# Second attention layer: the row of maxima is placed ahead of the step's scores, and copied ahead of the step's exponent

## The reference, cut to what matters

```python
q = q * scale
attn = jnp.einsum('bqd,bkd->bqk', q, k)
attn = (attn.reshape(B * nh, H, W, H, W) + rel_h[:, :, :, :, None] + rel_w[:, :, :, None, :]).reshape(B * nh, N, N)
attn = jax.nn.softmax(attn, axis=-1)
out = jnp.einsum('bqk,bkd->bqd', attn, v)
...
x = x + _L0_conv_ref(_gn(x), ...)
x = x + _L1_conv_ref(_gn(x), ...)
```

## Time and profile before

| | us |
|---|---|
| median of 3 runs | 3359.76 |
| lowest, highest | 3355.78, 3362.64 |
| the profiled execution's own time | 3359.43 |
| its span, first to last instruction | 3357.2 |
| PE busy | 2895.1 (86%) |
| DVE busy | 2494.8 (74%) |
| POOL busy | 1903.2 (57%) |
| ACT busy | 1862.9 (55%) |

### The profile page before, as it was taken

One profiled execution on the slowest core, in us unless ns is written; L12 is line 12 of the kernel. 1 busy time (PEld: TensorE's weight loads), 2 busy tenths in 40 slices (PEclk: granted clock), 3 DMA queues, 4 the chain that ended last, 5 costly groups with the idle time before them and its releaser, 6 DMA issues. The chain is left out here.

```text
span 3357.2 us, 94851 instructions
## 1 busy us (share of the span) xinstructions
PE 2895.1 (86%) x34200; PEld 1947.2 (58%) x34200; DVE 2494.8 (74%) x5171; ACT 1862.9 (55%) x3434; POOL 1903.2 (57%) x1561
## 2 busy tenths in 40 slices
PE   1996999997199748999999999999999999999977
PEld 1554677773155625666666666666666666666644
DVE  6745888876654537888787888888888888888854
ACT  3333666774333425666565666656565666566654
POOL 3452555550303006777777777777777777777762
PEclk9996999998599559999999999999999999999989
DMA  2425565547121984222222222222222222222114
GB/s 115 178 87 132 139 145 132 139 117 258 45 119 58 245 185 136 49 50 50 50 50 50 50 50 50 50 50 53 47 58 48 56 49 56 46 57 59 22 41 142
DMA packets 162461, 294.95 MB, mean 88 GB/s; under 512 B 78522, under 2 KB 112404, under 8 KB 156564
## 3 DMA queue, kind: packets, MB, share of 16 engines
q1 hardware_dynamic: 162052, 289.43, 33.9%
HBM read 189.37 MB, written 85.45 MB: 82 GB/s over the span
## 5 line engine op out<-in xcount | busy, mean ns | idle before, releaser
L1704 POOL TENSOR_TENSOR fprob_low<-fprob 128x768 f16<-128x768 f32 x1008 | 1449.7, 1466 | 563.3 <-ACT fprob L1672 562.8
L1715 DVE TENSOR_REDUCE fpart_max<-fmax_acc 128x1 f32<-128x384 f32 x2592 | 1363.8, 556 | 368.7 <-PE fmax_acc L1543 353.0
L1672 ACT ACTIVATE fprob<-fscores 128x768 f32<-128x768 f32 x1296 | 1048.2, 809 | 768.7 <-PE fscores L1572 768.6
L1543 PE MATMUL fmax_acc<-fk_m,fq_m 128*128 128x384 f16 x2592 | 853.2, 330 | 146.0 <-ACT fq_b L1660 104.8
L1570 PE MATMUL fscores<-fq_a,fk_a 128*128 128x384 f16 x2592 | 848.2, 327 | 39.5 <-issue 31.5
L1572 PE MATMUL fscores<-fq_b,fk_b 97*128 97x384 f16 x2592 | 851.4, 328 | 4.2 <-issue 4.2
L1596 PE MATMUL fout_acc<-fv,fprob 128*128 128x65 f16 x7776 | 612.0, 191 | 2.6 <-POOL fprob_low L1704 2.1
L1597 PE MATMUL fout_acc<-fv,fprob_low 128*128 128x33 f16 x7776 | 596.0, 179 | 0.9 <-issue 0.9
L1596 PEld LDWEIGHTS fout_acc<-fv,fprob 128*128 128x128 bf16 x7776 | 543.2, 97 | 68.4 <-POOL fprob_low L1704 5.1
L1597 PEld LDWEIGHTS fout_acc<-fv,fprob_low 128*128 128x128 f16 x7776 | 487.9, 96 | 52.5 <-issue 2.6
L1543 PEld LDWEIGHTS fmax_acc<-fk_m,fq_m 128*128 128x128 f16 x2592 | 251.9, 97 | 336.7 <-DVE fpart_max L1715 121.1
(11 more groups left out here) (128 smaller groups left out, 3834.9 us busy)
## 6 DMA issues: line engine op xcount, KB each, us to landing
q_a<-q_hi SPq DMA_DIRECT2D x48, 432.0 KB, 5.7
fq_a<-q_hi SPq DMA_DIRECT2D x48, 432.0 KB, 7.6
q_a<-q_lo SPq DMA_DIRECT2D x24, 432.0 KB, 7.4
row_bias<-x SPq DMA_DIRECT2D x24, 432.0 KB, 7.7
col_bias<-x SPq DMA_DIRECT2D x72, 144.0 KB, 3.8
fq_a<-q_lo SPq DMA_DIRECT2D x24, 432.0 KB, 8.6
fq_a<-col_bias SPq DMA_DIRECT2D x24, 432.0 KB, 11.9
fq_b<-row_bias SPq DMA_DIRECT2D x24, 432.0 KB, 14.6
```

The source lines that it names most:

```text
L1543: nc.tensor.matmul(max_acc[:, piece_bank(g, u, j), 0:PIECE], q_m[:, b, tile * 128:(tile + 1) * 128], k_m[:, b, piece * PIECE:(piece + 1) * ...
L1672: nc.scalar.activation(prob[:, k % RING, :].rearrange("p (j n) -> p j n", j=2), scores[:, 2 * (k % 2):2 * (k % 2) + 2, 0:UNIT], ACT.Exp).t ...
L1704: engine.tensor_tensor(prob_low[:, k % RING, :], prob[:, k % RING, :], prob[:, k % RING, :].bitcast(BF16)[:, 1::2], ALU.subtract).then_inc ...
L1715: nc.vector.reduce_max(part_max[:, u % 2, j // PIECES, j % PIECES:j % PIECES + 1], max_acc[:, piece_bank(g, u, j), 0:PIECE], axis=AX.X).th ...
```

## The change

In `attention_full`, at step 7 of a unit, PE's `row_of_max` stands ahead of `scores_of` instead of behind it, and ACT's `place_row` stands ahead of `exps` instead of behind it. The waits are the same ones, written at the same operations. A function is renamed.

```diff
@@ PE, stage
                 for k in range(STEPS):
-                    scores_of(n, b, k)
-                    coming = row_after(n, k)
+                    coming = row_of(n, k)
                     if coming:
                         row_of_max(*coming)
+                    scores_of(n, b, k)
@@ ACT, stage
                 for k in range(STEPS):
-                    exps(n, k)
-                    coming = row_after(n, k)
+                    coming = row_of(n, k)
                     if coming:
                         place_row(*coming, b if coming[1] else 1 - b)
+                    exps(n, k)
```

More of the change, by code:

```diff
@@ L1433, in piece_bank, with row_of @@
         return (u + j + (1 if j < 2 else 0)) % 2
-    def row_after(n, k):
+    def row_of(n, k):
         unit = k // PAIRS + 1
```

## The result

| | before | after |
|---|---|---|
| median | 3361.2 us of 4 runs (3355.78 to 3367.49) | 3284.74 us of 4 runs (3281.58 to 3286.59) |
| the profiled execution's own time | 3359.43 us | 3281.58 us |
| its span | 3357.2 us | 3279.3 us |

The ratio is 0.9771, with a 95% interval of 0.9752 to 0.9790: the change makes the kernel faster by 76.5 us by the medians and by 77.9 us between the two profiled executions. Forecast were 79.8 us and 3280 us.

The account below looks back on a forecast made before the run. PE was taken to bound the kernel. Per unit 0.90 - 0.32 = 0.58 us; 132 x 0.58 + 10 x 0.32 = 79.8 us off 3359.4 gave 3280 us, range 3270 to 3305.

Parts of the forecast that it names:

- The bubble of 0.90 us: Before piece 3 in step 7, PE loses 0.90 us per unit because the row's copy stands behind the exponent on ACT.
- The new wait of 0.32 us: At step 7's start, PE's row now waits 0.32 us for DVE's read of piece 0, which uses the same bank.
- The ten late units: In one unit of twelve, ten in all, DVE reads piece 0 later: wait 0.58 us, gain 0.32 us.
- The copy ends 0.48 us before piece 3: On ACT in step 7, the row is copied 0.48 us before piece 3, so the old bubble goes entirely.
- the exponent of step 7 is 0.49 us later and delays nobody: On ACT, it starts 0.49 us later but ends 0.34 us before DVE's low half needs it.
- DVE, POOL and ACT do not become the bound: In a unit of 12.8 us, DVE has 11.2 us of work, POOL 9.8 and ACT 8.2, all below.
- The sum: Over the loop and other units, 132 x 0.58 + 10 x 0.32 = 79.8 us gained, giving 3280 us.
- B: Rival: the row at step 7 does not wait for DVE; gain 128 us, 3231 us; chance 0.03.
- D: Rival: late DVE makes the row wait over 0.90 us, holding up the scores; slower, 3436 us; chance 0.04.
- C: Rival: part of the gain is given back at a new PE wait downstream, half the 0.58 us; 3320 us; chance 0.11.
- E: Rival: no effect, the copy is earlier but piece 3 waits for something else as long; 3360 us; chance 0.04.
- ACT's margin of 0.18 us: In step 7 on ACT, the copy is over 0.18 us before the exponent's scores are ready.

Follow-up runs that it names:

- Experiment 2: ACT's half alone against the kernel before: the copy ahead of the exponent, the row's products left behind the scores; 3282.51 us, ratio 0.9756.
- experiment 5: Changed kernel with the row's two waits in the other order, DVE's reads first; 3290.14 us in one profiled execution, not compared.
- experiment 3: Against the kernel before: row's products between the two tiles of step 7's scores, copy ahead of the exponent; 3249.63 us, on another occasion (again) 3254.54 us.
- experiment 8: Unread products added ahead of the first stage: 64 on the kernel of experiment 7, 3251.98 us; 6 on the changed kernel, 3293.74 us.
- experiment 4: Against the kernel before: row's products ahead of the second max piece of step 6, copy ahead of the exponent of step 7; 3332.08 us, ratio 0.9901.
- experiment 1: PE's half alone against the kernel before: the row's products ahead of the scores, the copy left behind the exponent; 3441.78 us, ratio 1.0230.
- experiment 6: Changed kernel with SP issuing the next stage's loads 24 steps later; 3285.01 us, ratio 0.9766.
- experiment 7: Edits of experiment 3 and experiment 6 together: row between the score tiles, copy ahead of the exponent, loads 24 steps later; 3243.80 us, ratio 0.9637.

## Why the prediction was right, point by point

- *The bubble of 0.90 us and its cause.* Right. The distance of the two max pieces of step 7 is 0.50 us after. Experiment 2 shows directly that the copy's place behind the exponent was the cause: moved alone, it recovers 0.67 us of a unit.
- *The new wait of 0.32 us for DVE's read of piece 0.* Right, to a hundredth, in the loop. In the written-out stages it is 0.41 us, 0.09 more, from the separate semaphore instruction (experiment 5), 2 us in all.
- *The ten late units.* Right: the row waits 0.57 us in one unit of each pass (0.58 was worked out), which is 0.25 us longer after, and was not before.
- *The copy ends 0.48 us before piece 3; the exponent of step 7 is 0.49 us later and delays nobody.* Right: the copy ends at 2007.42 and piece 3 starts at 2007.89; the exponent is over at 2008.40, and DVE's low half starts at 2008.73. ACT's margin is 0.17 us where 0.18 was worked out.
- *DVE, POOL and ACT do not become the bound.* Right, and with more to spare than assumed: experiment 3 runs a unit in 12.48 us, with PE still packed.
- *The sum.* 79.8 us against 77.9 between the profiled executions. The near hit is in part luck: PE's stretch in the second layer's attention became 75.5 us shorter (2001.2 to 1925.7), and 2.4 us came from outside it, where nothing was changed. By the distances between PE's products, the bubbles gave back some 128 us (forecast 127.8), the waits of the row took 49.5 (forecast 48.0), PE's stops in the loop took 6.3 us more than before, and the stretches at the lower clock took 2.5 less. The last two had no term in the sum; together they are some 4 us that were missed, and in experiments 2, 3 and 8 they are larger.
- *The rivals.* B, the row does not wait, fell with the trace of the changed kernel: the wait is there and the row starts 0.06 us after DVE's read, in experiment 4 as well. The rule of the Trainium skill named in the prediction ("PSUM — Partial Sum Buffer", section "PSUM bank collisions raise a hardware error") was kept in every version, since the semaphore stayed: no row starts before that read is over. No run here leaves the wait out, so none tests the rule. B's size, though, was real: 0.90 us a unit could be had, by asking for the row later and not earlier. D, slower, is what PE's half alone does (experiment 1), not for the reason that D gave, a late DVE, but because the scores are held up while the copy still stands behind the exponent. C's sign, a new wait for L1704 or L1672, did not come in the changed kernel, and E fell with the distance of 0.50 us.

Two things in the prediction's manner were weak. It priced the change's two halves only together, and so did not see that one of them was a loss in itself. And it put C on ACT's margin of 0.18 us; experiments 2 and 3 used that up, with the exponent of step 7 starting 0.02 to 0.03 us behind the copy, and PE met no new wait in its units.

## What to carry to other kernels

When a small producer, its copy and its consumer stand on three queues, look on each queue for what stands in front of it, and price each move alone: here the copy behind an exponent cost 0.90 us a unit, and moving the producer too early cost 0.32 of it again. The best place for an operation that waits for another engine is where the wait has just ended, and the trace of the old kernel gives that moment (0.26 + 0.06 us into the step). Measure a bubble by the distance of starts, as the idle column counted 0.75 us for a loss of 0.90, and 0.16 for one of 0.32.

## What the runs showed of the hardware that had not been expected

**The supply of instructions at a loop's turn.** In the kernel before, PE stops at each of the nine turns inside the loop for 3.5 to 4.0 us, and a 16 KB packet of the instruction queue q8 is moved meanwhile. (All stops are given from the start of one product to the start of the next.) Some turns of other versions take 4.5 to 5.6 us. In all of these, two 16 KB packets of q8 started around the last max piece, up to 1.4 us behind it, and the longer of the two took 1.4 to 2.7 us; a short stop of 3.4 to 4.3 us has only one, of 0.9 to 1.7 us. The kernels before and after and experiments 1, 4 and 6 had no long stop, experiment 2 had four turns of nine, experiment 3 five on the first occasion and nine on the second, experiments 5 and 7 nine. The queues in the stop, first one turn of the changed kernel, then one of the kernel of experiment 3 on its second occasion (packets, MB, share of 16 engines):

```profile
q8 instruction: 1, 0.02, 2.3%
q14 instruction: 3, 0.02, 2.1%
```

```profile
q8 instruction: 2, 0.03, 4.6%
q14 instruction: 4, 0.03, 2.3%
```

Twelve instructions more ahead of the loop brought the second packet to five turns of the changed kernel, and 128 more took it away from all turns of the other (experiment 8). That the place of the code matters is shown by these two; that the second packet is the next block of code behind the branch was only argued. The place is not all that decides: the same kernel had five long turns and nine in experiment 3, and experiment 2, with as many instructions as the changed kernel, has four.

**Stops where the loads run.** Stops of 1.1 to 2.3 us between two products of PE come where the loads move some 200 GB/s, and they move when the loads or the code are moved (experiments 6 and 8). Beside every one of them, in all versions, lies a 16 KB packet of q8 that started 0.2 to 1.9 us before the last product ahead of the stop, so the stops go with the fetch of code. That the loads hold up this fetch was only argued: the packets beside the stops took 1.2 to 1.6 us, and the middle one of the loop took 1.1 to 1.2.

**What the loop lost beside its units.** In the 120 units of the loop, each distance between two products was compared with the middle distance at the same place of a unit. The surplus in us, by what it goes with (the rest, 0.6 to 8.0 us, is in the total):

| kernel | stops at the turn | other stops over 0.9 | lower clock | total |
|---|---|---|---|---|
| before | 32.9 | 4.2 | 11.5 | 49.6 |
| changed | 32.2 | 11.2 | 9.0 | 55.6 |
| experiment 1 | 32.1 | 1.1 | 18.3 | 57.4 |
| experiment 2 | 36.8 | 8.8 | 20.7 | 66.9 |
| experiment 3 | 38.7 | 12.8 | 12.4 | 66.4 |
| experiment 3 again | 43.7 | 11.4 | 17.9 | 79.5 |
| experiment 4 | 32.9 | 9.7 | 14.7 | 59.8 |
| experiment 5 | 45.1 | 6.2 | 14.8 | 69.4 |
| experiment 6 | 33.4 | 3.8 | 11.2 | 56.5 |
| experiment 7 | 43.8 | 0.0 | 16.2 | 66.8 |
| experiment 8, 64 products | 32.3 | 24.4 | 12.4 | 70.2 |
| experiment 8, 6 products | 36.8 | 13.8 | 15.6 | 69.1 |

By the distances of the copies, a pass of the loop is 4.9 us longer than twelve plain units before, 5.4 in the changed kernel, and 5.5 to 7.9 in the others. Kernels with the same unit of 12.48 us (experiments 3, 7 and 8) took between 3243.80 and 3254.54 us.

**The clock after a stop.** Behind most of the stops at the turn (seven of nine before, six of nine after) some products ran at the 1.2 GHz level. The first of these stretches is such a stop in the changed kernel, the second what follows it, at a granted clock of 0.51. The bubbles of 0.90 us never had this effect: in the loop of the kernel before, the clock is at the lower level only behind the turns. The lower level cost 11.5 us there and 9.0 after, so 2.5 us of the gain between the profiled executions are the clock's and not the bubbles'; whether that is the change or chance is not shown.

```profile
2060.70:2064.20 3.50, 0.04 (x1) 0.00 (x0) 1.11 (x3) 0.22 (x1) 1.47 (x1) 1.00 0.05 12
2064.20:2067.70 3.50, 3.38 (x22) 1.87 (x23) 1.11 (x2) 0.81 (x1) 0.92 (x1) 0.51 0.03 7
```

**Two waits in front of one product** cost 0.09 us on PE where the one that is met later sits on a semaphore instruction of its own: the row then starts 0.147 us after DVE's read and not 0.058. In those units it is the wait that is written last; with the wait that is met later written first, the 0.09 us are gone (experiment 5).
